# A two-layer decoder on one core: new front order, paired exponentials at the end of the first attention, sums joined on VectorE in the second

## What is computed

```python
# L0_attn: softmax over exp(-distance), 256 x 256, per batch
x = _layernorm(x + _L0_attn_ref(x, ...))
# L0_xattn ("first attention" below): 16 heads of 8 channels
att  = causal softmax(q  @ k.T  * scale) @ v      # 256 x 256, on x itself
attc = softmax(qc @ kc.T * scale) @ vc            # 256 x 1601, on the context
x = _layernorm(x + (att + attc) @ Wp + bp)
# L0_ffn: 8 experts, top 2;  L1_attn: a complex linear recurrence
# L1_xattn ("second attention"): one head, 256 queries x 1601 context rows per batch
out = softmax(q @ k.T) @ v
# L1_ffn: gated, three matmul layers with gelu
```

## Time and profile before

| | |
|---|---|
| median of 3 runs | 651.18 us (650.05 to 654.44) |
| the profiled execution | 650.36 us |
| its span, first to last instruction | 648.5 us |
| mean granted TensorE clock | 0.987 of full speed |
| busy: PE, DVE, ACT, POOL | 603.2, 518.6, 448.7, 217.5 us |

### The profile page before, as it was taken

One profiled execution on the slowest core, in us unless ns is written; L12 is line 12 of the kernel. 1 busy time (PEld: TensorE's weight loads), 2 busy tenths in 40 slices (PEclk: granted clock), 3 DMA queues, 4 the chain that ended last, 5 costly groups with the idle time before them and its releaser, 6 DMA issues. The chain is left out here.

```text
span 648.5 us, 13664 instructions
## 1 busy us (share of the span) xinstructions
PE 603.2 (93%) x5214; PEld 333.1 (51%) x5214; DVE 518.6 (80%) x710; ACT 448.7 (69%) x818; POOL 217.5 (34%) x296
## 2 busy tenths in 40 slices
PE   9989999999999999999999999999729899999995
PEld 5644534444444444444433467777313566667884
DVE  5369999999999999999993369899599668787532
ACT  3555589999999999999998555555691355666214
POOL 8214334326666566766667002100000000023000
PEclk9999999999999999999999999999969999999999
DMA  8357596566655534435421036995000100000000
GB/s 209 114 145 219 192 276 181 157 172 171 168 158 155 149 81 116 92 85 121 104 57 32 2 108 224 317 319 174 1 0 1 49 1 1 1 1 0 1 1 32
DMA packets 44895, 71.11 MB, mean 110 GB/s; under 512 B 13048, under 2 KB 32544, under 8 KB 44832
## 3 DMA queue, kind: packets, MB, share of 16 engines
q1 hardware_dynamic: 31840, 38.34, 22.6%
q0 software_dynamic: 12384, 29.66, 13.9%
q10 hardware_dynamic: 608, 2.25, 1.6%
HBM read 44.68 MB, written 24.80 MB: 107 GB/s over the span
## 5 line engine op out<-in xcount | busy, mean ns | idle before, releaser
L1010 ACT ACTIVATE prob<-ps 128x512 f32<-128x512 f32 (+2 forms) x480 | 250.8, 584 | 24.1 <-PE ps L772 16.6
L1134 DVE TENSOR_REDUCE pm<-ps 128x2 f32<-128x1024 f32 x192 | 224.1, 1209 | 5.7 <-PE ps L730 5.6
L795 PE MATMUL ps<-prob,vst 128*9 128x256 f32 (+1 forms) x1664 | 132.1, 381 | 3.2 <-ACT o_all L998 3.2
L772 PE MATMUL ps<-qq,kc 50*128 50x256 bf16 (+1 forms) x832 | 131.8, 273 | 0.9 <-DMA qq<-mrow 0.9
L730 PE MATMUL ps<-kc,qq 48*128 48x512 bf16 x384 | 117.6, 383 | 1.3 <-DVE pm L1134 1.2
L772 PEld LDWEIGHTS ps<-qq,kc 50*128 50x128 bf16 (+1 forms) x832 | 52.0, 95 | 96.3 <-ACT prob L1010 79.0
L795 PEld LDWEIGHTS ps<-prob,vst 128*9 128x9 f32 (+1 forms) x1664 | 27.8, 88 | 44.8 <-ACT prob L1010 27.8
L718 PE MATMUL ps<-masks_b 64*128 64x256 bf16 x256 | 38.0, 269 | 0.0
L730 PEld LDWEIGHTS ps<-kc,qq 48*128 48x128 bf16 x384 | 34.1, 93 | 6.8 <-DVE pm L1134 3.6
L1474 ACT ACTIVATE sg<-ps,exp_bias 128x512 f32<-128x512 f32 x32 | 21.8, 685 | 20.2 <-PE ps L1388 20.2
L535 POOL TENSOR_TENSOR o_all<-o_all,below 128x512 f32<-128x512 f32 x14 | 17.8, 1269 | 50.6 <-DMA below<-rden_scr 50.5
(11 more groups left out here) (370 smaller groups left out, 1259.8 us busy)
## 6 DMA issues: line engine op xcount, KB each, us to landing
kc<-kc_scr SPq DMA_DIRECT2D x32, 300.2 KB, 4.5
below<-rden_scr POOLq DMA_DIRECT2D x14, 256.0 KB, 5.9
comb_bc<-comb_scr SPq DMA_DIRECT2D x7, 512.0 KB, 6.2
ctx<-ctx_scr POOLq DMA_DIRECT2D x4, 801.0 KB, 6.8
raw<-in_wexp POOLq DMA_DIRECT2D x8, 384.0 KB, 5.7
exp_scr<-raw_high POOLq DMA_DIRECT2D x8, 384.0 KB, 4.7
exp_scr<-raw_low POOLq DMA_DIRECT2D x8, 384.0 KB, 5.3
kc_scr<-hi SPq DMA_DIRECT2D x6, 400.2 KB, 4.8
```

The source lines that it names most:

```text
L772: last = pe.matmul(bank[0:p, j * TQ:(j + 1) * TQ], kc[s][rows, j, t * 128:t * 128 + p], qq[s][rows, 0, j, :], start=(j == 0), stop=True, s ...
L795: last = pe.matmul(o_ps[32 * hh:32 * hh + VW, kind * TQ + q0:(kind + 1) * TQ], value[:, hh * VW:(hh + 1) * VW], prob[0:k, (NST * n + t) % ...
L1010: act.activation(prob[0:p, g % P_RING, 2 * e:2 * e + 2, q0:TQ], s2[0:p, k % S2_RING, 0:2 * w].rearrange("p (i q) -> p i q", i=2), ACT.Exp, ...
L1134: dve.tensor_reduce(pm[:, m % 2, c, :, jt], banks, AX.X, ALU.max).then_inc(s1_read, 1)
```

## The change

Four edits.

1. Front. PE: `keys(4)` moves ahead of `pe_ln2(1)` (the second matmul of the layer norm of chunk 1) and `values(0)` behind it. ACT: `high(4)` moves ahead of `act_ln2(1)`, and from piece 5 on `high(j)` stands ahead of `middle(j-1)`. DVE: `rest(4)` moves ahead of `values(0)` and of the layer norm of chunk 1. SP: the cross query rows of batch 0 are written to scratch before the keys of unit 0 are read, and read back after half of the self query rows are written.
2. Last 20 steps of the first attention (g from 220): scores go to pairs of banks (6, 7) and (0, 1) in turn, with one exponential over both banks. Scores g wait for exponential g-2 (at g = 221 for exponential 220). The copy of unit 14's outputs comes after both heads' exponential of step 226, not between them.
3. The denominators of unit 14 go to the halves of bank 2, and DVE waits for both.
4. Second attention: DVE adds the two sides of `total` after p = 5, p = 6 adds to that, and PE makes one sum matmul in place of two. The counts of `added` follow.

```diff
@@ SP
                     sp.wait_ge(filled, 2 * SLOTS)
+                    split_out("qc", 0)
                     sp.wait_ge(*KEYS_OUT[0])
                     load_context(0)
-                    split_out("qc", 0)
-                    split_out("qs", 0)
+                    split_out("qs", 0, (0,))
                     load_split("qc", 0)
+                    split_out("qs", 0, (1, 2))
                     split_out("ks", 0)
@@ PE
                     pe_ln(1)
+                    keys(4)
+                    pe_ln2(1)
                     values(0)
-                    pe_ln2(1)
-                    keys(4)
                     keys(5)
@@ ACT
                     middle(3)
+                    high(4)
                     act_ln2(1)
-                    high(4)
                     for j in range(5, LATE_KEYS):
+                        high(j)
                         middle(j - 1)
-                        high(j)
@@ DVE
                     rest(3)
+                    rest(4)
                     values(0)
                     dve_ln(1)
-                    rest(4)
@@ first attention, definitions
+            PAIRED_FROM = (NU - 1) * NST - 5
+            def spread_out(n, kind):
+                return ps[:, 6 + kind, 0:TQ] if n == NU - 1 else ps[:, 2, kind * TQ:(kind + 1) * TQ]
+            def pair_at(g):
+                return (6, 0)[(g - PAIRED_FROM) % 2]
@@ scores_t
+                        if g >= PAIRED_FROM:
+                            if e == 0 and j == 0:
+                                if g == PAIRED_FROM:
+                                    pe.wait_ge(s1_read, HALVES * NU)
+                                else:
+                                    pe.wait_ge(exp_done, 2 * g if g == PAIRED_FROM + 1 else 2 * g - 2)
+                            bank = ps[:, pair_at(g) + e, :]
@@ ACT, steps
+                        if g >= PAIRED_FROM:
+                            act.wait_ge(av_done, g - P_RING + 1)
+                            act.wait_ge(s2_ready, 2 * g + 2)
+                            act.activation(prob[0:p, g % P_RING, :, q0:TQ].rearrange("p (e i) q -> p e i q", e=2),
+                                           ps[0:p, pair_at(g):pair_at(g) + 2, 0:2 * w].rearrange("p e (i q) -> p e i q", i=2),
+                                           ACT.Exp, scale=SCALE).then_inc(exp_done, 2)
+                            if t == 1 and n:
+                                copy_out(n - 1)
+                            continue
@@ last_normalise (DVE)
-                            dve.wait_ge(last_bc_ps, 2 * i + kind + 1)
+                            dve.wait_ge(last_bc_ps, 2 * i + (kind + 1 if n == NU - 1 else 2))
@@ second attention, PE
-                    pe.wait_ge(added, (PAIRS - 1) * (b + 1))
-                    for i in range(2):
-                        last = pe.matmul(fin[:, TQ:2 * TQ], ones[:], total[:, b % 2, i, :], start=(i == 0), stop=(i == 1))
-                    last.then_inc(fin_ps, 1)
+                    pe.wait_ge(added, PAIRS * (b + 1))
+                    pe.matmul(fin[:, TQ:2 * TQ], ones[:], total[:, b % 2, 0, :], start=True, stop=True).then_inc(fin_ps, 1)
@@ second attention, DVE (add)
+                    if p == PAIRS - 2:
+                        dve.wait_ge(added, PAIRS * b + p)
+                        dve.tensor_tensor(total[:, b % 2, 0], total[:, b % 2, 0], total[:, b % 2, 1], ALU.add).then_inc(added, 1)
```

More of the change, by code:

```diff
@@ L349, in load_context, with split_out @@
                                 "c r j t -> (c r) (j t)")).then_inc(slot_in[s], 16)
-                    def split_out(kind, b):
+                    def split_out(kind, b, parts=range(3)):
                         j = last_piece[groups.index((kind, b // 2))]
@@ L355, in split_out @@
                         rows = KPART if kind == "ks" else QPART
-                        for part, ready in enumerate(((j_hi, j + 1), (j_mid, j + 1), lows(j))):
+                        for part, ready in [(i, ((j_hi, j + 1), (j_mid, j + 1), lows(j))[i]) for i in parts]:
                             sp.wait_ge(*ready)
@@ L763, in scores_t @@
                     def scores_t(n, t, e, j):
-                        s, k = n % SLOTS, 2 * (NST * n + t) + e
-                        if j == 0 and k >= S2_RING:
-                            pe.wait_ge(exp_done, k - S2_RING + 1)
-                        bank = s2[:, k % S2_RING, :]
+                        s, g, k = n % SLOTS, NST * n + t, 2 * (NST * n + t) + e
+                        if g >= PAIRED_FROM:
[5 more added lines that the diff above has]
+                            bank = ps[:, pair_at(g) + e, :]
+                        else:
+                            if j == 0 and k >= S2_RING:
+                                pe.wait_ge(exp_done, k - S2_RING + 1)
+                            bank = s2[:, k % S2_RING, :]
                         rows = head_rows(e, KROWS)
@@ L866, in denominators @@
                                 pe.wait_ge(last_scaled, kind + 1)
-                            pe.matmul(ps[:, 6 + kind, 0:TQ], later["spread"][:], o_all[:, n, kind * TQ:(kind + 1) * TQ],
+                            pe.matmul(spread_out(n, kind), later["spread"][:], o_all[:, n, kind * TQ:(kind + 1) * TQ],
                                       start=True, stop=True).then_inc(last_bc_ps, 1)
@@ L1174, in last_normalise @@
                         for kind in range(2):
-                            dve.wait_ge(last_bc_ps, 2 * i + kind + 1)
-                            dve.reciprocal(last_bc[:, kind * TQ:(kind + 1) * TQ], ps[:, 6 + kind, 0:TQ]).then_inc(last_scaled, 1)
+                            dve.wait_ge(last_bc_ps, 2 * i + (kind + 1 if n == NU - 1 else 2))
+                            dve.reciprocal(last_bc[:, kind * TQ:(kind + 1) * TQ], spread_out(n, kind)).then_inc(last_scaled, 1)
                         dve.wait_ge(last_scaled, 3 * i + 2)
@@ L2096, in _ @@
                             before, step = divmod(k - RING, PAIRS)
-                            act.wait_ge(added, (PAIRS - 1) * before + max(step, 1))
+                            act.wait_ge(added, PAIRS * before + max(step, 1) + (step == PAIRS - 1))
                         m, w = (128, 2 * TQ) if p < PAIRS - 1 or NKT % 2 == 0 else (KLAST, TQ)
@@ L2288, in add @@
                     elif p:
-                        dve.wait_ge(added, (PAIRS - 1) * b + p - 1)
+                        dve.wait_ge(added, PAIRS * b + p - 1 + (p == PAIRS - 1))
                         rows, sides = (slice(0, 128), slice(0, 2)) if p < PAIRS - 1 else (slice(0, KLAST), slice(0, 1))
```

## The result

The changed kernel takes **646.13 us** (median of 20 runs, 644.87 to 648.45) against 651.4 of the kernel before in the same session; the ratio is 0.9922, with a 95% interval of 0.9905 to 0.9938. That is 0.8% less: a real gain, and within the 1% that the prediction called no change. Forecast were 647.2 us in a range of 644.3 to 649.8.

A forecast was written before the change was run, and what follows sets the result against it. DVE sets the pace mid first attention, PE and ACT alternate in its last steps, ACT's wait for DVE delays the front. 650.36 - 2.3 - 0.9 - 0.8 = 646.4, on the median's footing 647.2 us; range 644.3 to 649.8.

The forecast's parts named there:

- The bound in the front: Front, pieces 4 to 9: ACT idles 0.82 us ahead of `middle`, PE pays late; removing this gains 2.3 us.
- From there PE is the bound: four values of 0.90 and four keys of 0.94: Front from 35.63 us: PE's run puts `keys(9)` at about 43.9 and `rest(9)` at about 45.9.
- Is its data there?: Front: cross query rows land at 46.5 to 47.5 us, 0.7 to 1.7 ahead of PE, so covered.
- the front gives nothing: Rival, front: PE waits on SP's data instead of DVE, `half(0)` stays at 50.6; 649.5 us, chance 0.15.
- Last 20 steps: End of first attention: paired exponentials gain 1.6 us, waits cost 0.5 and 0.3; 0.9 us less taken.
- The wait at 221: Last steps: scores 221 wait for exponential 220, so ACT stands 0.5 us.
- The copy behind both exponentials: Step 226: copy of unit 14's outputs waits for the whole exponential, with PE and ACT behind it; costs about 0.3 us.
- two banks cost more than two instructions: Rival, every step from 220: a two-bank exponential takes 1.2 us on ACT; 652.1 us, chance 0.05.
- more than forecast: Rival: front gains 3.4 us, last steps 1.8, sums of the second attention 1.8; 644.2 us, chance 0.12.
- the edits don't reach the end: Rival, expert block: weights arriving at their own time give back gains won before 364 us; near 650.3 us, chance 0.05.
- Second attention: Sums: two rows fewer gain 0.44, 0, 0.40 and 0 us at batches 0 to 3; 0.8 taken.
- + 0.40: Second attention, batch 2: the sum ends sooner, the join nearly hidden in DVE's idle time; gain of 0.40 us.

The follow-up runs named there:

- The first experiment: Changed kernel with SP's queue put back in its old order, the new orders of PE, ACT and DVE kept: 650.18 us, ratio 0.9985 to the kernel before.
- the second experiment: Kernel before with SP's queue alone in the new order: 650.92 us, ratio 0.9992.
- run 320: Not a run: in "the pairs run 320 us later" run is a verb; the paired exponentials act some 320 us after the kernel's start.

## Why the prediction was right, and where it was off

- **The bound in the front** (idle time of ACT ahead of each `middle`, passed on to PE and DVE): right. The idle time ahead of `middle` is gone for four of the six pieces and half for the other two, `half(0)` hangs on the same `rest(9)` and last values, 3.0 us sooner, at 47.65 where 48 to 49 was the sign of being right. Mis-sized was "From there PE is the bound: four values of 0.90 and four keys of 0.94". These are durations of rows; from start to start a values row takes 0.74 and a keys row 0.86, a pair 1.60, since each begins before the last one's end. So PE was through with its run sooner and waited 0.85 us for `rest(7)` on DVE; `keys(9)` came at 43.32 and `rest(9)` at 45.30, not at 43.9 and 45.9. That is 0.6 of the 0.74 us between 2.3 and 3.04; 0.1 more is what the prediction took off its own 2.4 for DVE's low parts.
- **"Is its data there?"**: the landing was forecast at 46.5 to 47.5 and came at 47.44, but the 0.7 to 1.7 us of cover had shrunk to 0.2, since PE was sooner. The text spoke of what the data would cost if late as "what it lands late". The first experiment shows two things that it left out: without the SP edit the data would have been 2.2 us late, so this edit, which by itself changes nothing, decides over nearly the whole gain; and a wait of 2.2 us costs 3.6, through the clock.
- **Rival "the front gives nothing"**: refuted, but its mechanism (PE waiting on SP's data) is what the first experiment made. It was 0.2 us away.
- **Last 20 steps**: 0.91 against 0.9, and that near agreement is luck: gains put at 1.6 came to 2.17, and costs put at 0.8 came to 1.26. The exponential was right (1038 ns forecast, 1027 measured), and so was 0.93 us a step as a mean. "So ACT remains the bound" does not hold in steps 228 to 231, where ACT waits for PE; and the largest single gains are not the 0.066 of a step but 0.26 into the step before the last, 0.21 behind each of two projections (0.3 was given for both together) and 0.21 on the way to the copy. The wait at 221 cost 0.66 against the kernel before, and 0.74 by the run that takes it away, instead of 0.5. The copy behind both exponentials cost 0.54 instead of 0.3: the chain that the text names (outputs, denominators and scores behind the copy, ACT behind those) is the one that the rows show, with PE standing 1.10 us, and only its size was off. With the wait gone and the copy ahead, the piece is 2.36 us shorter than before (24.28 against 26.64).
- **Rival "two banks cost more than two instructions"**: refuted by the rows of 1.01 to 1.05 us. By the Trainium skill, page "ScalarE: Activation LUTs", section "What ACT_TABLE_LOAD costs", an ACTIVATE takes 186 ns + 0.833 ns a column; the estimate from this for 1024 columns is 1039 ns, and the measured mean over two banks is 1027.
- **Rival "more than forecast"**: its front came almost (3.04 of 3.4); the last steps (0.91 of 1.8) and the sums (0.4 of 1.8) did not.
- **Rival "the edits don't reach the end"**: no sign of it; the piece with the expert block is 0.28 us shorter, not longer.
- **Second attention**: 0.44, 0 and 0.40 at batches 0 to 2 were right to 0.03 us. The step that failed is "+ 0.40" for batch 2 as a gain at the end: the text checked that the reciprocal came sooner and not what batch 3 waits for. That is ACT, which runs without idle time from the batch's first exponential to its sixth, timed by the copy of `shift` ahead of the sum's end: 10.56 us before, 10.57 after. The 0.44 is given back. The sum is 0.4, not 0.8.
- **The sum**: edits 4.3 us against 4.0 forecast, where 0.7 more in the front and 0.4 less in the second attention offset each other; the interval of the ratio, 4.0 to 6.2 us around the 5.3 between the medians, holds both.

## What to carry to other kernels

When a compute engine is made faster ahead of a point that also needs data, look at the landing time of that data in the trace before: the difference to the engine's arrival is all the gain that there is, until the queue is reordered too. Price a wait of TensorE for data with what the clock loses behind it. And when a chain is shortened, name what the next stage waits for: an engine that runs there without idle time, from a start that the shortened chain doesn't move, takes the gain back.

## What the runs showed of the hardware

- **The start costs 1.5 us more in some executions.** The first piece was 32.75 to 33.09 us in nine of the fourteen profiles and 34.46 to 34.78 in five, with none between. In these five PE waits 0.94 to 1.00 us at 10 us for DVE, and the clock is 0.65 to 0.72 in the window from 12 to 16 us; but the second experiment's execution had the same wait and a clock of 1.00, so the wait alone does not settle it. The five are all of kernels with the pairs, as are five of the other nine; the pairs run 320 us later, and whether the program's other layout has a part in it stays open, as does the cause. The 20 runs of the changed kernel lie 3.6 us apart; how many of them have this is not known, since only one was profiled.
- **A lone stall of 0.2 to 0.6 us** in a run of eight outputs between 86 and 91 us, in four of the fourteen profiles (before among them, where the row takes 1.05 instead of 0.62 us). It explains the -0.45 of the third piece: in the ten profiles without it the piece takes 285.7 to 285.8. Its cause stays open. One such row:

```profile
87.22 1.24 PE L814 MATMUL ps<-prob,vst 128*9 128x256 f32 x8
```

- **The expert block varies by up to 2 us between executions, and the variation is PE's wait for weights.** From the first to the last of its 32 steps on DVE it takes 69.1 to 71.0 us, once 73.2. In eleven of the fourteen profiles two waits of PE that a DMA ends (0.59 to 1.60 and 0.73 to 1.71 us) are all that differs: without them the block takes 68.03 to 68.05. Before, the first of the two is

```profile
417.42 0.47 PE L1386 MATMUL ps<-x_high,up_high 128*128 128x512 f32 x1 [1.60 <-DMA exp_bias<-in_wexp]
```

The two are 2.47 us together before and 2.14 after, which holds the -0.28 of the fifth piece. The ten kernels with the pairs lie at 69.1 to 70.7 and the four without at 70.5 to 73.2, so a part of the edits in it can't be excluded; why the weights land sooner or later stays open. An effect under 1 us in this kernel can be seen in the pieces of a trace and not in six runs.
